# Four-layer model on one core: the third layer's feed-forward on rows sorted by expert

## The chip, the core and the metric

The kernel runs on one core of a Trainium2 chip. The metric is the time of one execution in microseconds (us), taken on the device. A core has a matrix engine (TensorE, PE), a vector engine (VectorE, DVE), a scalar engine (ScalarE, ACT), a general engine (GpSimd, POOL), and SyncE (SP), which here issues transfers. Each runs its own list of instructions in order; they wait for each other by semaphores.

## The reference

Four layers, numbered 0 to 3. In each the attention's output is multiplied by the SiLU of a feed-forward's output and added to x. Each layer has an attention and a feed-forward of its own kind. The ones that the change touches are those of layer 2, the third:

```python
# one layer: x = x + attention(layernorm(x)) * silu(feed_forward(layernorm(x))), for four layers
# x is (2, 1024, 128), FP32
def _L2_attn_ref(x, Wqkv, Wproj, bproj):
    ...
    qkv = qkv.reshape(b, n, N_HEADS, -1)
    q, k, v = (qkv[..., :dh], qkv[..., dh:2 * dh], qkv[..., 2 * dh:])
    scores = jnp.einsum('bnhd,bngd->bnhg', q, k) / SCALE
    attn = jax.nn.softmax(scores, axis=-1)
    out = jnp.einsum('bnhg,bngd->bnhd', attn, v)
    out = out.reshape(b, n, -1)
    return jnp.einsum('bni,mi->bnm', out, Wproj) + bproj

def _L2_ffn_ref(x, tile_sigs, W, b):
    ...
    pe = make_pe(S, P)
    scores = jnp.einsum('sp,tp->st', pe, jnp.sign(tile_sigs))
    idx = jnp.argmax(scores, axis=-1)
    y_all = jnp.einsum('bsd,tod->bsto', x, W) + b
    ...
    out = jnp.take_along_axis(y_all, idx4, axis=2)[:, :, 0]
    return out
```

The attention of layer 2 is a softmax over 16 heads within each position, so every position stands alone. Its feed-forward multiplies each position by one of eight 128x128 matrices. Which one follows from the position's number alone and is the same in both halves of the batch. Layers 0, 1 and 3 have feed-forwards in which the tokens choose among eight experts (two of them in 0 and 1, one in 3). Layer 3's attention is a causal product with a decay, without a softmax.

## The kernel before

The 2048 positions lie as 16 tiles of 128, in four chunks c = 0 to 3 of 512 columns (two for each half h of 1024 positions). There is one function for each engine, and in it a generator for each stage. `follow()` reads a string of words for each engine (`ORDER_A`, `SIDE_B` beside layer 0's attention, then `ORDER_C`); a word such as `ffn2.1` or `tile.12` runs that stage up to its next `yield`. These strings, written out, are the only thing that sets the order on an engine. Waits name what is waited for (`at("xnT", 2, c)`), and PSUM banks come from a ring of three, banks 4, 6 and 7.

The routed feed-forwards (layers 0, 1 and 3) work on sorted rows, in six groups: q = 0, 1 for layer 0, q = 2, 3 for layer 1, q = 4, 5 for layer 3, each a half of the positions. For a group DVE computes for every token its expert and its place in the sorted order (`route.q`, in it `counted`), and POOL scatters the normalised rows to the DRAM buffer `xsort` with indirect transfers, 128 rows each. SP loads them in tiles of 256 rows (`xrows.q`). PE transposes a tile (`xturn.q`), multiplies it by the weights of the experts of its two halves of 128 rows (`up.q`, `down.q`), and SP stores the results to `ysort` (`store.q`). Then POOL gathers each token's rows back with indirect transfers (`gather.q`), and ACT applies the SiLU. Sorted rows are padded so that each half of a tile has one expert. SP also loads the experts' weights, by a number read from the table `rt`.

The feed-forward of layer 2 works differently, by masked products. `position` computes a one-hot choice for the 1024 positions, split into three bf16 parts, in `gTT2`. `ffn2.c` runs over the eight experts of a chunk. PE spreads the row of the one-hot over 128 partitions (bf16, 128x512), DVE multiplies it with the normalised activations (`psum_sb<-xnT,ps`), and PE multiplies the product by the expert's matrix and adds up in bank 5 (`ps<-psum_sb,on_sb`). Three bf16 products add the bias, and ACT applies the SiLU into `gT`. `end2.c` then multiplies the attention's output by `Wproj`, DVE adds `bproj` and multiplies by `gT`, four transposes on PE turn the result, and DVE adds it to x.

The attention of layer 2 runs in 16 stages `tile.i`. PE makes q, k and v; ACT copies them out; DVE forms the products of q and k (128x2048) and sums them to scores (128x256) with their maxima; POOL subtracts the maxima (the shift, 128x256); ACT takes the exponential; DVE forms the shares; POOL makes the products with v in four instructions (128x512, printed 128x4x16x8 in an order listing); PE sums them over 16 transposes (`sum_turned`); and ACT copies the result. The small buffers of a tile (q, k, v, scores, maxima) are one of two, as are the two large ones of products `pr1` and `pr2`. So the sums of tile i wait for POOL's products of tile i - 2.

Normalisation of chunk c ahead of layer l is `ln.l.c`: DVE takes moments, POOL forms the offsets, ACT scales, PE transposes, ACT copies to `xnT`. In PE's, DVE's and POOL's helpers each operation has one line: 255 is a matmul, 258 a transpose, 261 a summed transpose, 264 a tensor_tensor, 277 a reduction, 280 a cast, 298 ACT's copy, 301 its activation, 304 a transfer of SP, 318 a scatter, 323 a gather, 331 a weight load by number. A few names in the profile stand for several buffers that share memory: `ar` is a large area with most of the layers' buffers, `on_sb` holds the eight matrices of layer 2.

## Time and profile before

| | |
|---|---|
| runs | 1004.75 us median of 3 (1003.81 to 1006.44) |
| profiled execution | 1003.7 us from its first to its last instruction |
| PE busy | 920.3 us, 92% |
| DVE busy | 764.0 us, 76% |
| POOL busy | 597.9 us, 60% |
| ACT busy | 538.3 us, 54% |
| moved | 97.17 MB, 97 GB/s in the mean |

The profile gives the busy time of an engine, the duration of each instruction, and what it waited for. A row of a timeline has the start, the duration, the engine and the line, the operation with output and inputs, how many of it were joined (x4), and in brackets the idle time ahead with what ended it. "Issue" is time in which the engine waited for nothing that the profile shows. The granted clock is the part of TensorE's full clock that it was given in a stretch.

### The profile page before, as it was taken

The numbers are of one execution on the slowest core, as the hardware profiler recorded it, in microseconds if no ns is written. First come the engines' busy times: TensorE is split into PE (matmuls) and PEld (weight loads), VectorE is DVE, ScalarE is ACT, GpSimd is POOL, SyncE is SP. The second block draws the span as 40 slices with busy tenths as digits, with TensorE's granted clock in tenths as the row PEclk, the third lists the DMA queues.
The fourth block names the chain that finished last, engine by engine and source line by source line (L and its number), as shares of the span: only waits on it lengthen the run. The fifth ranks groups of instructions, "written<-read, shape, count | busy, mean of one in ns | idle before, by whom it ended". The sixth has DMA issues, their size and how long they took to land. (4 is left out here: it accounts for less than half of the span.)

```text
span 1003.7 us, 20954 instructions
## 1 busy us (share of the span) xinstructions
PE 920.3 (92%) x7704; PEld 489.4 (49%) x7713; DVE 764.0 (76%) x1332; ACT 538.3 (54%) x901; POOL 597.9 (60%) x533
## 2 busy tenths in 40 slices
PE   5799997999999999999989997899889787799997
PEld 3346563233333333333323233798788444488794
DVE  6978888888888889887888825883689998873514
ACT  1255345666766666666756775443266243274463
POOL 3660425788778777887777893123735886652333
PEclk9999998999999999999999999799999997999999
DMA  9372525111111101111101123567651200243462
GB/s 319 137 225 88 153 64 156 41 51 46 26 52 28 58 24 49 34 55 56 35 26 44 40 67 116 161 193 241 225 156 35 89 22 22 79 142 101 143 196 79
DMA packets 92308, 97.17 MB, mean 97 GB/s; under 512 B 23184, under 2 KB 68624, under 8 KB 91952
## 3 DMA queue, kind: packets, MB, share of 16 engines
q1 hardware_dynamic: 87088, 85.34, 27.8%
q0 software_dynamic: 5120, 10.50, 3.6%
q8 instruction: 63, 1.03, 0.4%
q14 instruction: 37, 0.30, 0.1%
HBM read 70.57 MB, written 24.77 MB: 95 GB/s over the span
## 5 line engine op out<-in xcount | busy, mean ns | idle before, releaser
L255 PE MATMUL ps<-ar 64*64 64x512 bf16 (+5 forms) x5312 | 538.6, 448 | 17.7 <-ACT ar L301 4.3
L255 PEld LDWEIGHTS ps<-ar 64*64 64x64 bf16 (+2 forms) x5312 | 268.5, 137 | 273.4 <-ACT ar L301 92.0
L277 DVE TENSOR_REDUCE small<-ps 128x2 f32<-128x1024 f32 (+2 forms) x276 | 307.2, 1140 | 52.0 <-PE ps L255 50.6
L301 ACT ACTIVATE ar<-ps 128x1024 f32<-128x1024 f32 (+1 forms) x304 | 285.4, 941 | 113.1 <-PE ps L255 106.5
L264 POOL TENSOR_TENSOR psum_sb<-psum_sb,ar 128x1024 f32<-128x1024 f32 x91 | 214.8, 2360 | 57.3 <-DVE on_sb L264 47.1
L264 POOL TENSOR_TENSOR ar<-ar 128x512 f32<-128x512 f32 (+1 forms) x80 | 79.2, 995 | 52.1 <-DVE ar L277 30.0
L323 POOL DMA_INDIRECT gT<-ysort,rt x48 | 46.9, 977 | 98.7 <-issue 97.7
L264 DVE TENSOR_TENSOR ar<-ps,ar 128x256 f32<-128x256 f32 (+4 forms) x56 | 56.2, 1011 | 47.9 <-PE ps L255 43.4
L264 POOL TENSOR_TENSOR psum_sb<-ar 128x1024 f32<-128x1024 f32 x32 | 75.9, 2372 | 16.8 <-ACT ar L301 15.6
L298 ACT COPY ar<-ps 128x256 f32<-128x256 f32 (+1 forms) x84 | 31.8, 386 | 80.8 <-PE ps L255 50.2
L255 PE MATMUL ps<-wA,xnT 128*128 128x512 f32 (+3 forms) x192 | 62.0, 447 | 5.3 <-DVE ar L264 2.7
L255 PE MATMUL ps<-ar,onesf 128*32 128x512 f32 x384 | 61.0, 593 | 0.7 <-DVE psum_sb L264 0.6
L255 PE MATMUL ps<-ar,psum_sb 128*128 x464 | 59.6, 277 | 1.1 <-DVE ar L264 0.8
L255 PEld LDWEIGHTS ps<-ar,psum_sb 128*128 128x128 f32 x464 | 56.0, 192 | 7.9 <-issue 7.6
L318 POOL DMA_INDIRECT xsort<-ar,rt x32 | 35.4, 1105 | 36.3 <-DVE rt L280 27.9
L298 ACT COPY lrow<-ps 128x512 f32<-128x512 f32 x32 | 18.8, 586 | 66.1 <-PE ps L255 66.1
L277 DVE TENSOR_REDUCE ar<-ar 128x16 f32<-128x256 f32 (+1 forms) x48 | 49.6, 1038 | 5.2 <-ACT ar L301 4.4
L255 PE MATMUL ps<-ar,ps_sb 128*128 x96 | 48.7, 602 | 0.0
L318 POOL DMA_INDIRECT xsort<-acc_sb,rt x32 | 32.5, 1016 | 20.5 <-DVE rt L280 11.1
L255 PEld LDWEIGHTS ps<-wA,xnT 128*128 128x128 f32 x192 | 29.5, 200 | 26.6 <-issue 12.0
L255 PE MATMUL ps<-on_sb,wA 128*32 128x512 f32 x256 | 35.0, 618 | 6.0 <-DVE on_sb L264 4.6
L255 PE MATMUL ps<-psum_sb,on_sb 128*128 128x512 f32 x64 | 34.4, 620 | 6.1 <-DVE psum_sb L264 5.1
(156 smaller groups left out, 1066.0 us busy)
## 6 DMA issues: line engine op xcount, KB each, us to landing
ar<-in_L_up SPq DMA_DIRECT2D x48, 384.0 KB, 4.1
ar<-in_L_b SPq DMA_DIRECT2D x32, 322.0 KB, 3.4
rec_sb<-lscr SPq DMA_DIRECT2D x64, 128.0 KB
scr<-ar SPq DMA_DIRECT2D x48, 128.0 KB, 2.1
ar<-xsort SPq DMA_DIRECT2D x40, 128.0 KB
ysort<-ar SPq DMA_DIRECT2D x40, 128.0 KB, 3.3
ar<-scr SPq DMA_DIRECT2D x32, 112.0 KB
xsort<-xs SPq DMA_DIRECT2D x12, 256.0 KB, 6.2
```

Of the source, the lines that this page charges most:

```text
L255: return self.e.matmul(o, l, r, start=start, stop=stop) if self.e else Nothing()
L264: return self.e.tensor_tensor(o, a, b, op) if self.e else Nothing()
L277: return self.e.tensor_reduce(o, a, AX.X, op, negate=True) if negate else self.e.tensor_reduce(o, a, AX.X, op)
L298: return self.e.copy(o, a) if self.e else Nothing()
L301: return self.e.activation(o, a, fn, **kw) if self.e else Nothing()
L318: return self.e.indirect_dma_start(rows, bass.IndirectOffsetOnAxis(ap=index, axis=0), i, None)
L323: return self.e.indirect_dma_start(o, None, rows, bass.IndirectOffsetOnAxis(ap=index, axis=0))
```

## The change

Layer 2's feed-forward now works on sorted rows as well. `position` gives a one-hot of the choice, PE forms the ranks from it and DVE the places (`counted("pos")`), once for both halves. `scatter2.h` on POOL sends the normalised rows of a half to the new DRAM buffer `xsort2` in eight scatters. `xrows2.h` on SP loads them in eight tiles of 256 rows, `xturn2.h` on PE turns a tile and reads the numbers of its two experts into registers, ACT copies it (`xout2.h`), `ffn2.h` makes two FP32 and two bf16 (bias) products of 128x128, ACT copies the rows (`rows2.h`), SP stores them to `ysort2` (`store2.h`), and `gather2.h` on POOL brings them back in eight gathers, behind which ACT applies the SiLU. So 16 scatters, 16 row loads, 16 stores and 16 gathers come in. The masked products on DVE and PE and the spreads go. `end2.c` makes its products with the positions on the partitions, with `bproj` added by a bf16 product, so that the transposes and one step of DVE go. The bias rows come through three small transfers `bias2` on SP. Eight transfers of 256 KB clear `xsort2` at the start of the program. The 256 KB load of the spreading table and a clearing on POOL are dropped.

In the attention of layer 2 the small buffers are a ring of three; q is read from PSUM and no longer kept, while the two large buffers stay two. The sums of tile i then wait for the products of tile i - 3. The normalised rows of layer 2 are written to `psum_sb`, which has two buffers, since the masked products are gone from it.

`ORDER_A` and `SIDE_B` are the same word for word. `ORDER_C` is another for every engine. The lines of the helpers lie four further down (259 a matmul, 262 a transpose, 268 a tensor_tensor, 308 a transfer of SP, 322 a scatter, 327 a gather, 314 the reading of numbers on PE).

```diff
+TILES2 = ((1024 + NE * (HALF - 1)) // HALF + 1) // 2
...
-STRIDE = (256, 384, None, 512)
+STRIDE = (256, 384, 128, 512)
...
-        "tile.12 route.4 tile.9 tile.10 ffn2.3 ffn2.2 ffn2.2 route.4 ffn2.2 ffn2.3 tile.11 att3.0 tile.13 ffn2.3 "
...
+        "gather2.1 gather2.1 gather2.1 gather2.1 gather2.1 gather2.1 tile.13 gather2.1 tile.12 tile.13 tile.13 tile.13 "
...
-            pe.mm(ps[:, b, :], wA[:, 384:512], oT2[c % 2]).then_inc(*filled(b, ("proj2", c)))
-            yield
-            combine(2, c, acc_sb[:, 1024:1536])
+            pe.wait_ge(*at("bias_rows_in", 0))
+            for j in range(4):
+                d_ = ps[:, b, 128 * j:128 * j + 128]
+                pe.mm(d_, oT2[c % 2][:, 128 * j:128 * j + 128], wA[:, 384:512], stop=False)
+                ins = pe.mm(d_, onesb[0:3, :], bias_rows[0:3, 1024:1152], start=False)
+            ins.then_inc(*filled(b, ("delta", 2, c)))
...
-        def ffn2(c):
-            x_ = slice(CW * (c % 2), CW * (c % 2) + CW)
-            pe.wait_ge(*at("xn", 2, c))
-            pe.wait_ge(*at("gT", "pos"))
-            for e8 in range(NE + 1):
-                if e8 < NE:
-                    b = take(ring[0])
-                    pe.wait_ge(*vacant(b))
-                    pe.mm(ps[:, b, :], cb_late[:, 128 * e8:128 + 128 * e8], gTT2[:, x_]).then_inc(
-                        *filled(b, ("spread", c, e8)))
-                    if e8:
-                        yield
-                if e8 == 1:
-                    pe.wait_ge(*vacant(5))
-                if e8 >= 1:
-                    p = e8 - 1
-                    pe.wait_ge(*at("xb", c, p))
-                    pe.mm(ps[:, 5, :], w2l[:, 128 * p:128 * p + 128],
-                          psum_sb[:, 512 * (p % 2):512 * (p % 2) + 512], start=p == 0, stop=False).then_inc(
-                        *up(("xb_used", c, p)))
-                if e8 < NE:
-                    yield
-            pe.wait_ge(*at("bias2", 0))
...
+            pe.wait_ge(*at("pos_dve", "chosen"))
+            pe.mm(ps[:, b, 0:64], below, ohs[:, 0:64])
+            pe.mm(ps[:, b, 128:192], onesb, ohs[:, 0:64]).then_inc(*filled(b, ("ranks", "pos")))
...
+        def x_turned2(h):
+            for J in range(TILES2 * h, TILES2 * h + TILES2):
+                b = take(ring[0])
+                pe.wait_ge(*vacant(b))
+                pe.wait_ge(*at(f"xsort2_in{J % 3}", J))
+                for k in range(2):
+                    ins = pe.tr(ps[:, b, 128 * k:128 * k + 128], xin2[J % 3][:, 128 * k:128 * k + 128], ident)
+                ins.then_inc(*filled(b, ("xT2", J)))
+                pe.wait_ge(*at("experts", "pos"))
+                j = 2 * (J % TILES2)
+                number2[J] = pe.numbers(nc, experts["pos"][0:1, j:j + 2], (NE - 1) * STRIDE[2])
+                yield
+
+        number2 = {}
+
+        def ffn2(h):
+            for J in range(TILES2 * h, TILES2 * h + TILES2):
+                b = take(ring[0])
+                pe.wait_ge(*vacant(b))
+                pe.wait_ge(*at("xT2_sb", J))
+                pe.wait_ge(*at("late_in", 0))
+                pe.wait_ge(*at("bias_rows_in", 0))
+                for k in range(2):
+                    d_ = ps[:, b, 128 * k:128 * k + 128]
+                    pe.mm(d_, xT2[J % 2][:, 128 * k:128 * k + 128], w2l[:, bass.ds(number2[J][k], 128)], stop=False)
+                    ins = pe.mm(d_, onesb[0:3, :], bias_rows[0:3, :][:, bass.ds(number2[J][k], 128)], start=False)
+                ins.then_inc(*filled(b, ("yrow2", J)))
+                yield
 
...
-            dve.wait_ge(*at("proj2", c))
-            dve.wait_ge(*at("ffn_act", 2, c))
-            if c > 0:
-                dve.wait_ge(*at("delta", 2, c - 1))
-            dve.stt(acc_sb[:, 1024:1536], ps[:, bank["proj2", c], :], M("bp"), gT[:, cols(c)], ALU.add,
-                    ALU.mult).then_inc(*emptied(("proj2", c), ("gated", 2, c)))
-            yield
-            combine(2, c)
+            blend(2, c)
...
-        def ffn2(c):
-            x_ = xnT[:, cols(c)]
-            for e8 in range(NE):
-                if e8:
-                    yield
-                xb = psum_sb[:, 512 * (e8 % 2):512 * (e8 % 2) + 512]
-                dve.wait_ge(*at("spread", c, e8))
-                if e8 >= 2:
-                    dve.wait_ge(*at("xb_used", c, e8 - 2))
-                elif c > 0:
-                    dve.wait_ge(*at("xb_used", c - 1, e8 + 6))
-                dve.tt(xb, x_, ps[:, bank["spread", c, e8], :], ALU.mult).then_inc(
-                    *emptied(("spread", c, e8), ("xb", c, e8)))
...
+            counted("pos")
...
             dve.wait_ge(*at("qk", i))
-            if i >= 2:
-                dve.wait_ge(*at(f"tile{k}_pool", i - 2, "av"))
+            if i >= 3:
+                dve.wait_ge(*at(f"tile{r}_pool", i - 3, "av"))
             dve.red(s, p1, ALU.add).then_inc(*up((t, i, "scores")))
...
+        def x_out2(h):
+            for J in range(TILES2 * h, TILES2 * h + TILES2):
+                act.wait_ge(*at("xT2", J))
+                if J >= 2:
+                    act.wait_ge(*at("yrow2", J - 2))
+                else:
+                    act.wait_ge(*at("scaled", 30))
+                act.acp(xT2[J % 2], ps[:, bank["xT2", J], 0:TILE]).then_inc(*emptied(("xT2", J), ("xT2_sb", J)))
+                yield
+
+        def rows2(h):
+            for J in range(TILES2 * h, TILES2 * h + TILES2):
+                act.wait_ge(*at("yrow2", J))
+                if J >= 2:
+                    act.wait_ge(*at(f"ysort2_out{J % 2}", J - 2))
+                else:
+                    act.wait_ge(*at("scaled", 30))
+                act.acp(yrow2[J % 2], ps[:, bank["yrow2", J], 0:TILE]).then_inc(
+                    *emptied(("yrow2", J), ("yrow2_sb", J)))
+                yield
+
+        def gather2(h):
+            for c in range(2 * h, 2 * h + 2):
+                for i in range(4 * (c % 2), 4 * (c % 2) + 4):
+                    act.wait_ge(*at(f"rows2_in{i}", h))
+                act.af(gT[:, cols(c)], gT[:, cols(c)], ACT.Silu).then_inc(*up(("gather_act",), ("ffn_rows", 2, c)))
...
+        def scatter2(h):
+            pool.wait_ge(*at("experts", "pos"))
+            pool.wait_ge(*at(f"clear{h}_in", 0))
+            for i in range(8):
+                c = 2 * h + i // 4
+                pool.wait_ge(*at("xnT", 2, c))
+                pool.scatter(xsort2[h], slots["pos"][:, i:i + 1], lnbuf(2, c)[:, 128 * (i % 4):128 * (i % 4) + 128]
+                             ).then_inc(*landed(("sorted2", h) if i == 7 else ("sorted2",)))
+                yield
+
+        def gather2(h):
+            for J in (TILES2 * h + TILES2 - 2, TILES2 * h + TILES2 - 1):
+                pool.wait_ge(*at(f"ysort2_out{J % 2}", J))
+            for i in range(8):
+                pool.wait_ge(*at("x", 2, 2 * h + i // 4))
+                pool.gather(gT[:, 128 * (8 * h + i):128 * (8 * h + i) + 128], ysort2[h], slots["pos"][:, i:i + 1]
+                            ).then_inc(*landed((f"rows2_in{i}", h)))
+                yield
...
+            for r in range(0, TILES2 * TILE, 512):
+                sp.dma(xsort2[h][r:r + 512, :].rearrange("(p t) d -> p t d", p=128), xs[:, 0:4, :]).then_inc(
+                    *landed((f"clear{h}_in",)))
...
+        def bias2():
+            sp.wait_ge(*at("bias2", 0))
+            sp.wait_ge(*at("scaled", 31))
+            for i in range(3):
+                sp.dma(bias_rows[i:i + 1, 0:1152], bp2[i][0:9, :]).then_inc(
+                    *landed(("bias_rows_in", 0) if i == 2 else ("bias_rows_in",)))
+            yield
+
+        def x_rows2(h):
+            sp.wait_ge(*at("sorted2", h))
+            for J in range(TILES2 * h, TILES2 * h + TILES2):
+                r = TILE * (J - TILES2 * h)
+                if J >= 3:
+                    sp.wait_ge(*at("xT2", J - 3))
+                sp.dma(v3(xin2[J % 3], 128), xsort2[h][r:r + TILE, :].rearrange("(k p) d -> p k d", p=128)).then_inc(
+                    *landed((f"xsort2_in{J % 3}", J)))
+                yield
+
+        def store2(h):
+            for J in range(TILES2 * h, TILES2 * h + TILES2):
+                r = TILE * (J - TILES2 * h)
+                sp.wait_ge(*at("yrow2_sb", J))
+                sp.dma(ysort2[h][r:r + TILE, :].rearrange("(k p) d -> p k d", p=128), v3(yrow2[J % 2], 128)).then_inc(
+                    *landed((f"ysort2_out{J % 2}", J)))
                 yield
 
```

Three places in the order. The first is SP's, where it passes from group 2 to group 3 (`ysort<-ar` is a store, `ar<-xsort` a load of sorted rows, `in_L_up` the experts' weights). Before:

```order
L304 DMA ysort<-ar 128x2x128
L304 DMA ar<-xsort 128x2x128 x2
L304 DMA ysort<-ar 128x2x128
L329 TENSOR_LOAD rt
L331 ISA
L331 DMA ar<-in_L_up 128x768
L329 TENSOR_LOAD rt
L331 ISA
L331 DMA ar<-in_L_up 128x768
L304 DMA ysort<-ar 128x2x128
```

After the change:

```order
L333 TENSOR_LOAD rt
L335 ISA
L335 DMA ar<-in_L_up 128x768
L308 DMA ar<-xsort 128x2x128 x3
L308 DMA ysort<-ar 128x2x128 x2
L308 DMA ar<-xsort 128x2x128 x2
```

The last two stores of group 2 stood apart, with row and weight loads of group 3 between and ahead of them; now they stand together behind three row loads.

The second is POOL's, around the scatters of `route.4` (`xsort<-rec_sb,rt` and `xsort<-lrow,rt`; a 128x256 row is the shift of a tile, the 128x4x16x8 rows are products with v). Before:

```order
L264 TENSOR_TENSOR ar<-ar 128x4x16x8 x4
L264 TENSOR_TENSOR ar<-ar 128x256
L318 DMA xsort<-rec_sb,rt 3072x128 x4
L318 DMA xsort<-lrow,rt 3072x128 x4
L264 TENSOR_TENSOR ar<-ar 128x4x16x8 x4
L264 TENSOR_TENSOR ar<-ar 128x256
L264 TENSOR_TENSOR ar<-ar 128x4x16x8 x4
```

After the change:

```order
L268 TENSOR_TENSOR ar<-ar 128x4x16x8 x4
L268 TENSOR_TENSOR ar<-ar 128x256
L322 DMA xsort<-rec_sb,rt 3072x128 x4
L322 DMA xsort<-lrow,rt 3072x128 x4
L268 TENSOR_TENSOR ar<-ar 128x4x16x8 x2
L327 DMA gT<-ysort,rt 128x128 x7
L268 TENSOR_TENSOR ar<-ar 128x256
L327 DMA gT<-ysort,rt 128x128
L268 TENSOR_TENSOR ar<-ar 128x4x16x8 x6
```

The scatters of `route.4` keep their place after the shift of tile 12. Behind them, seven gathers of `gather2.1` (`gT<-ysort,rt`) stand in the middle of tile 12's four products, and one behind tile 13's shift.

The third is PE's, around the rank products of `route.4` (`ps<-rt,cb`). `ps<-osb,ar` is a spread and `ps<-psum_sb,on_sb` a masked product; in the change `ps<-cf,acc_sb` turns a sorted tile, `ps<-on_sb,rec_sb` and `ps<-osb,cb` are its product and its bias, TENSOR_LOAD and ISA read the experts' numbers. Before:

```order
L255 MATMUL ps<-wA,xnT 128x8 x8
L261 MATMUL ps<-cf,ar 128x128 x32
L255 MATMUL ps<-osb,ar 128x512 x2
L255 MATMUL ps<-psum_sb,on_sb 128x512
L255 MATMUL ps<-rt,cb 128x64 x2
L255 MATMUL ps<-psum_sb,on_sb 128x512
L255 MATMUL ps<-osb,wA 128x512 x3
```

After the change:

```order
L265 MATMUL ps<-cf,ar 128x128 x32
L262 MATMUL ps<-cf,acc_sb 128x128 x2
L314 TENSOR_LOAD rt
...
L259 ISA
L259 MATMUL ps<-on_sb,rec_sb 128x128
L259 ISA
L259 MATMUL ps<-osb,cb 128x128
L259 MATMUL ps<-rt,cb 128x64 x2
L262 MATMUL ps<-cf,acc_sb 128x128 x2
```

Behind the 32 summed transposes of two tiles, the ranks stood behind two spreads and one masked product. Now three tiles of `xturn2.1` and three of `ffn2.1` stand ahead of them.

## Rows read from the trace of the kernel before

**Rows 1.** The profile's page: busy time by engine, and a line of its DMA issues.
```profile
PE 920.3 (92%) x7704; PEld 489.4 (49%) x7713; DVE 764.0 (76%) x1332; ACT 538.3 (54%) x901; POOL 597.9 (60%) x533
...
ysort<-ar SPq DMA_DIRECT2D x40, 128.0 KB, 3.3
```

**Rows 2.** Busy time by stretch: PE, PEld, DVE, ACT, POOL, then clock, DMA share, GB/s.
```profile
738.50:782.51 44.01, 41.73 (x305) 35.56 (x308) 41.76 (x59) 26.41 (x50) 26.86 (x30) 1.00 0.34 96
782.51:865.28 82.77, 60.65 (x267) 35.62 (x271) 76.42 (x136) 28.64 (x56) 58.69 (x67) 0.94 0.11 33
...
878.77:948.06 69.29, 69.23 (x468) 56.54 (x469) 38.18 (x90) 38.01 (x103) 26.88 (x32) 1.00 0.40 121
948.06:997.30 49.24, 48.97 (x338) 40.16 (x336) 13.13 (x27) 26.77 (x91) 15.15 (x16) 1.00 0.50 147
```

**Rows 3.** Timeline of POOL, 702 to 745: start, duration, instruction, idle time ahead.
```profile
702.92 1.00 POOL L323 DMA_INDIRECT gT<-ysort,rt  x1 [14.92 <-issue]
...
722.71 1.84 POOL L323 DMA_INDIRECT acc_sb<-ysort,rt  x1 [0.30 <-issue]
...
738.50 0.62 POOL L264 TENSOR_TENSOR ar<-ar 128x256 f32<-128x256 f32 x1 [11.55 <-DVE ar L277]
742.17 2.23 POOL L264 TENSOR_TENSOR ar<-ar 128x512 f32<-128x512 f32 x2 [3.05 <-DVE ar L264]
```

**Rows 4.** The chain of waits, 683 to 703: start, duration, what.
```profile
687.05 3.10 DMA xsort<-ar,rt
...
694.89 5.00 DMA ysort<-ar
```

**Rows 5.** Timeline of SP, its DMA issues, 690 to 700.
```profile
690.17 0.90 SPq L304 DMA_DIRECT2D ar<-xsort  x2
...
699.31 0.38 SPq L304 DMA_DIRECT2D ysort<-ar  x1
```

**Rows 6.** Instructions by line and shape, 738 to 866: count, busy us, mean ns, idle ahead.
```profile
L264 POOL TENSOR_TENSOR ar<-ar 128x512 f32<-128x512 f32 x48 | 52.0, 1083 | 16.0 <-DVE ar L264 13.6
...
L264 DVE TENSOR_TENSOR psum_sb<-xnT,ps 128x512 f32<-128x512 f32 x26 | 17.3, 678 | 2.1 <-remote 2.1
...
L264 POOL TENSOR_TENSOR ar<-ar 128x256 f32<-128x256 f32 x13 | 8.5, 654 | 23.5 <-DVE ar L277 23.4
L323 POOL DMA_INDIRECT acc_sb<-ysort,rt x8 | 8.4, 1050 | 3.5 <-issue 3.5
```

**Rows 7.** Instructions on the tile psum_sb, 745 to 900: durations min/median/max.
```profile
L255 PE MATMUL ps<-psum_sb,on_sb x64: 592/592/1061, 766.0 to 890.5; 128*128 128x512 f32 x64
...
L264 DVE TENSOR_TENSOR psum_sb<-xnT,ps x32: 658/679/689, 754.8 to 883.9; 128x512 f32<-128x512 f32 x32
```

**Rows 8.** Timeline of POOL, 865 to 881.
```profile
865.28 1.10 POOL L318 DMA_INDIRECT xsort<-rec_sb,rt  x1 [3.26 <-DVE rt L280]
...
874.27 0.95 POOL L318 DMA_INDIRECT xsort<-lrow,rt  x1 [0.30 <-issue]
875.24 5.13 POOL L264 TENSOR_TENSOR ar<-ar 128x512 f32<-128x512 f32 x5
```

**Rows 9.** Timeline of PE, five places between 695 and 911.
```profile
695.47 1.50 PE L255 MATMUL ps<-ar,psum_sb 128*128 x12
...
728.78 0.63 PE L258 MATMUL ps<-cf,rec_sb 128*128 128x128 f32 x4 [4.30 <-ACT rec_sb L301]
...
834.89 3.62 PE L261 MATMUL ps<-cf,ar 128*128 128x128 f32 x16
...
875.93 1.12 PE L255 MATMUL ps<-psum_sb,on_sb 128*128 128x512 f32 x2
...
908.51 1.91 PE L261 MATMUL ps<-cf,ar 128*128 128x128 f32 x16
```

**Rows 10.** The chain of waits at the end, 995 to 999.
```profile
995.94 2.62 DMA gT<-ysort,rt
```

**Rows 11.** Busy time and granted clock, 835 to 840; columns as in Rows 2.
```profile
835.00:840.00 5.00, 4.95 (x22) 4.17 (x22) 2.82 (x3) 3.46 (x7) 3.73 (x6) 0.60 0.10 40
```

More of the change, by code:

```diff
@@ L867, in tail0 @@
                 yield
-        def combine(layer, c, a):
-            b = take(ring[0])
-            pe.wait_ge(*vacant(b))
-            pe.wait_ge(*at("gated", layer, c))
-            for j in range(4):
-                ins = pe.tr(ps[:, b, 128 * j:128 * j + 128], a[:, 128 * j:128 * j + 128], ident)
-            ins.then_inc(*filled(b, ("delta", layer, c)))
         def end0(c):
@@ L1133, in tensor_program @@
                   "end0": end0, "end1": end1, "end2": end2, "tables": tables, "rec": rec, "position": position,
[L1134 removed]
+                  "ffn2": ffn2, "xturn2": x_turned2, "tile": tile, "att3": att3, "end3": end3, "route": route}
         follow(ORDER_A["tensor"], stages)
@@ L2278, in pool_program @@
         beside(attention(), SIDE_B["gpsimd"], {"end0": end0, "ln": ln, "route": route, "gather": gather})
-        follow(ORDER_C["gpsimd"], {"clear2": clear2, "ln": ln, "tile": tile, "route": route, "gather": gather})
+        follow(ORDER_C["gpsimd"], {"scatter2": scatter2, "gather2": gather2, "ln": ln, "tile": tile, "route": route, "gather": gather})
     def sync_program(sp):
```

166 lines of the change are left out of this document (62 added, 104 removed), and 268 rows, old and new, of tables (ORDER_A, ORDER_C, SIDE_B).

## The prediction

> **What bounds the kernel now.** I read the page first: TensorE (PE) is busy 92% of the span [rows 1]. That says where most work is, not what the new feed-forward is worth, for the edits lie after about 613 us. So the table of stretches comes next [rows 2]. From 738.50 to 865.28, where the sixteen attention tiles of layer 2 run, VectorE (DVE) is busy 41.8 + 76.4 = 118.2 of 126.8 us, PE 102.4 and GpSimd (POOL) 85.6: DVE is the bound. From 878.77 to 997.30 PE is busy 118.2 of 118.5 us: layer 3 is bound by PE. What joins the two is found in POOL's timeline: its scatters for the first expert group of layer 3 (`route.4`) begin at 865.28, the eighth starts at 874.27, and PE has the first sorted rows at 878.77, where the next stretch of the table begins [rows 2, 8]. The last 6.4 us are the tail of gathers. So I time three places: G, the first gather of group 2 (702.92) [rows 3], S, the first `route.4` scatter (865.28), and the end. G to S is 162.4 us, S to the end 138.4.
>
> **What goes and what comes, by engine.** DVE loses 32 products of 0.679 us, 21.8 us [rows 7]; 26 of them (17.3 us) stand between 738 and 866 [rows 6]. PE loses the 64 FP32 products behind them, 0.592 us each by the record [rows 7], though two are done in 1.12 us, 0.56 each [rows 9]: about 35 us, and 32 bf16 spreads. It gets back 32 transposes, 32 FP32 products of 128x128 and 32 bf16 ones: at 0.12 us each (sixteen in 1.91 [rows 9]) some 12 us. POOL gets 16 scatters and 16 gathers. Eight issues from 865.28 to 874.27 are 1.28 us apart [rows 8], sixteen from 702.92 to 722.71 are 1.32 apart [rows 3]; an undisturbed one takes 0.95 and the gap of 0.30 behind it, 1.25. That is 40 us, or 42 by the dearest spacing. ScalarE (ACT) gets 32 copies of 128x256, under 0.5 us each, against 71.7 us without work between 738.50 and 865.28 [rows 2]; SP's queue has the room as well. The eight clearing transfers at the very start delay weight loads used tens of microseconds later; I cost them at nothing, and up to 2 us if that cover is gone.
>
> **Step 1, G: -6.0 (from -9 to -2).** Now the last two stores of group 2 stand on SP behind rows and weights of group 3: SP asks for those rows at 690.17 and issues the last store at 699.31; 3.6 us later, at 702.92, POOL starts [rows 3, 5]. The last `down.2` stands behind group 3's first tile on PE (the product at 695.47 [rows 9]). In the changed order both last `down.2` precede `xturn.3`, and SP holds three row loads and then both stores. From 690.15, where the scatters have landed (687.05 + 3.10 [rows 4]), that is 1.4 us for three loads (0.45 each [rows 5]), 0.9 for two stores, a landing between 3.3 (the page's median [rows 1]) and 5.0 (this place [rows 4]), so 4.15, and 0.3: 696.9, that is 6.0 earlier. It is -2 if PE's last `down.2` comes 4 us later than I think, and -9 with the short landing and PE ready before the row loads are asked for.
>
> **Step 2, G to S: +7.7, from 162.4 to 170.1.** S stands behind all of POOL's work in one queue, so it is POOL's chain that counts. Before: 35.6 us from G to tile 0's shift; from there 85.6 busy, 5.4 of gaps at sixteen gathers (3.5 of them at the eight into acc_sb [rows 6]), and 2.0 of gaps under 0.3 us: 93.0 of work, and 33.8 idle. Most of the idle time is put down to DVE's maxima (23.4) and shares (13.6, a part inside the small gaps) [rows 6]. After: the first four scatters fit into the 11.55 us that POOL waits before tile 0's shift [rows 3]; on DVE that tile's steps stand behind two more steps of the expert feed-forward, which gives the shift 2.5 us later, 38.1 after G. Of the other 28 indirect transfers 20 stand before S: 20 x 1.25 = 25.1 us, so 118.1 of work. If POOL never idled, S would come at G + 156. Walking through both orders with the durations of these rows, I still find it waiting 3.1 for tile 0's shares (as the 3.05 at 742.17 [rows 3]), 3.2 at tile 1, 1.2 for the last stores before `gather2.0`, 1.6 at tile 11, 2.7 for the slots of `route.4` (3.26 now [rows 8]) and 2.1 in short waits: 13.9 in all, with 8 and 20 as its ends. 38.1 + 118.1 + 13.9 = 170.1. The slots come late for a reason of order: on PE the rank product of `route.4` now stands behind three `xturn2.1` and three `ffn2.1`, which need the last scatter of `scatter2.1`, and everything behind that product on PE waits with it. The time that DVE loses is thus no gain by itself: it shortens a wait of POOL's, and POOL's added work takes that wait's place. The ring of three lets DVE's sums run a tile further ahead of POOL's products; its effect is in the 13.9.
>
> An issue beside a busy DVE may be dearer: the eight gathers into acc_sb in the tile stretch take 1.05 us [rows 6], an undisturbed one 0.95, so 0.1 x 20 = 2 us. I take none of it, since most of the new ones stand in runs of three to eight. The dearest single one took 1.84 us [rows 3]. The Trainium skill, "SBUF — State Buffer", section "Who interferes with whom", speaks against this change: GpSimd can't write the descriptors of its DMA while VectorE holds the port pair that they share. By its figure of 620 ns becoming 3100 ns, twenty issues would add about 50 us, an estimate from that page. The trace shows the effect at 0.1 us in the mean and doesn't bear the figure out.
>
> **Step 3, S to the end: +1.1, from 138.4 to 139.5.** PE is saturated here, so its own work and new holes count. Of the old feed-forward six products stand behind `xturn.4`, 6 x 0.56 = 3.4, with a spread and the combining transposes 1.2 more; the new form of `end2` gives 0.7 back: -3.9. The tail loses 1.5: group 5's gathers lie fully under the last attention step of layer 3, where before their landing of 2.62 us came after PE's work [rows 10]. Holes: POOL issues seven `gather2.1` between the two halves of tile 12's product, where before all four and the next shift ran on from 875.24 [rows 8]. That is 7 x 1.25 = 8.8 us; PE comes to tile 12's transposes 21.9 after S and has them 25.4 after: +3.5. `ln.3.2` stands between PE's steps so that its rows come late; one such lateness cost 4.30 at 728.78 [rows 9], nothing is the other end, and I take 2.0. Layer 3's attention is spread differently, +1.0 (0 to 1.7). Sum: -3.9 - 1.5 + 3.5 + 2.0 + 1.0 = +1.1.
>
> **Sum.** -6.0 + 7.7 + 1.1 = +2.8 on a span of 1003.7: 1006.5. The median of the runs (1004.75) stands 1.0 above the profiled span, so 1007.5.
>
> **The rivals.**
> *A, the forecast:* POOL becomes the bound of the tile stretch, 1007.5, own range 1002 to 1012. Chance 0.41.
> *B, faster:* POOL's 33.8 idle us take in the 25.1, for they are waits for DVE, which has 17 us less to do. It decides when POOL idles no more than 6 us there: S is again 162.4 after G. If the holes at tile 12 and `ln.3.2` aren't there either, the later tiles being ready sooner, the end moves by -3.9 - 1.5 + 1.0 = -4.4: 1004.75 - 6.0 - 4.4 = 994.3. For it: 33.8 exceeds 25.1. Against: a part of the waits is the way from DVE to POOL to ACT and back within a tile, which no work taken from DVE shortens. Chance 0.28.
> *C, slower by the clock:* between 738.50 and 865.28 PE was busy 102.4 of 126.8 us, and with 25 less it is near 60%. Where it was least busy, the granted clock from 835 to 840 was 0.60, and sixteen summed transposes took 3.62 us against 1.91 [rows 9, 11]. If the lower level (1.2 GHz) holds at the rank product, the first tiles of layer 3 and tile 12, 7 us of such work take 7 more: 1014.5. Against: at other times before S PE has cover. Chance 0.16. The Trainium skill, "TensorE: Matmul & The Clock Gate", section "Part 1: The HAM clock gate (the "warmup" mystery)", puts it so: "the default state is throttled, and activity releases the throttle". The row at 835 agrees.
> *D, nothing:* the earlier G is used up, since the tiles wait for DVE's normalisation and not for POOL's queue; -3.9 - 1.5 stand against +3.5 + 2.0 in the end: about 1004. Chance 0.12.
> *E, issues blocked by DVE:* at the dearest row, 1.84 against 0.95, twenty of them add 17.8: 1025. Against it stands the mean. Chance 0.03.
>
> **The numbers.** A measurement of this kernel tells 0.3%, 3 us, from no change. Faster than 1001.7: B 0.27 and 0.06 of A and D, 0.33. Slower than 1007.8: A 0.15, C 0.15, E 0.03, 0.33. Between: 0.34. The range takes in the centres of B and C: 993 to 1015.
>
> **What would show it.** The last `ysort` store of group 2 issued by 694 and G near 697; between tile 0's shift and S POOL with 118 us of work and 12 to 16 idle, S at 866 to 870, DVE under 85% busy; seven `gather2.1` before tile 12's last products, with PE idle some 3 us there. The forecast is wrong if an indirect transfer costs over 1.3 us, if POOL still idles 25 us (S is then past 878) or under 8, or if the stretch's granted clock falls below 0.8.

## The result, and the profile after

The changed kernel takes 1047.14 us (median of 4, 1045.08 to 1049.8) against 1004.28 for the one before beside it (1003.76 to 1006.44): ratio 1.0433, 95% interval 1.0415 to 1.0451. The forecast was 1007.5, with a range to 1015. Its profiled execution spans 1046.7 us, 43.0 more than before. Of the page:

```profile
span 1046.7 us, 21211 instructions
...
PE 932.0 (89%) x7751; PEld 509.0 (49%) x7751; DVE 750.9 (72%) x1308; ACT 550.9 (53%) x933; POOL 628.7 (60%) x564
...
PEclk9899998999999999999999999989996667999899
```

DVE has less work than before, POOL more, as intended. PE has 12 us more, for 7751 products and transposes against 7704 [rows 1], many of them short ones. The last line is the granted clock in 40 slices of the span, in tenths; it has a hollow of 0.6 in the slices 31 to 33, from 785 us on. The page of the kernel before has 0.9 and more in those slices and nothing under 0.7 anywhere:

```profile
PEclk9999998999999999999999999799999997999999
```

The same three places as in the forecast: G is at 696.73, S at 883.70, the end at 1046.7. SP's queue ahead of G, and POOL's queue at three places (start, duration, operation, idle time ahead and what ended it):

```profile
691.90 1.41 SPq L308 DMA_DIRECT2D ar<-xsort  x3
693.35 0.98 SPq L308 DMA_DIRECT2D ysort<-ar  x2
```

```profile
732.79 0.62 POOL L268 TENSOR_TENSOR ar<-ar 128x256 f32<-128x256 f32 x1 [4.48 <-DVE ar L281]
...
800.73 5.68 POOL L268 TENSOR_TENSOR ar<-ar 128x512 f32<-128x512 f32 x4 [7.35 <-PE ps L265]
...
875.02 5.12 POOL L268 TENSOR_TENSOR ar<-ar 128x512 f32<-128x512 f32 x5 [2.58 <-DVE ar L268]
...
883.70 1.00 POOL L322 DMA_INDIRECT xsort<-rec_sb,rt  x1 [3.57 <-DVE rt L284]
885.01 0.96 POOL L322 DMA_INDIRECT xsort<-rec_sb,rt  x1 [0.30 <-issue]
```

| | before | forecast | after |
|---|---|---|---|
| G | 702.92 | 696.9 | 696.73 |
| G to S | 162.4 | 170.1 | 187.0 |
| S to the end | 138.4 | 139.5 | 163.0 |

So step 1 came out in its number, step 2 is short by 16.9 us and step 3 by 23.5. The table of stretches (length; busy time of PE, PEld, DVE, ACT, POOL; granted clock, DMA share, GB/s) shows both. Below it stand PE's longest waits ahead of S, and DVE's steps (`ps<-ps,gT` and `xs<-xs,ps`, the multiplication and the addition to x) that end the two longest:

```profile
883.70:903.30 19.60, 18.43 (x77) 12.85 (x77) 5.42 (x11) 4.34 (x12) 12.80 (x13) 0.74 0.63 196
903.30:1041.10 137.80, 124.03 (x797) 100.33 (x796) 54.30 (x116) 69.50 (x198) 48.34 (x54) 0.96 0.37 109
732.79:792.00 59.21, 51.69 (x357) 42.80 (x356) 44.84 (x59) 31.32 (x65) 42.42 (x46) 0.92 0.45 141
792.00:883.70 91.70, 51.88 (x244) 39.03 (x244) 61.40 (x110) 29.84 (x65) 62.46 (x72) 0.70 0.15 43
```

```profile
807.73 3.67 PE L265 MATMUL ps<-cf,ar 128*128 128x128 f32 x16 [2.55 <-DVE ar L268]
...
828.30 1.12 PE L262 MATMUL ps<-cf,psum_sb 128*128 128x128 f32 x4 [10.14 <-DVE xs L268]
...
843.23 1.65 PE L259 MATMUL ps<-wA,xnT 128*128 128x384 f32 x2 [11.49 <-DVE xs L268]
...
856.92 3.68 PE L265 MATMUL ps<-cf,ar 128*128 128x128 f32 x16 [5.95 <-DVE ar L268]
```

```profile
826.82 0.70 DVE L268 TENSOR_TENSOR ps<-ps,gT 128x512 f32<-128x512 f32 x1 [6.73 <-ACT gT L305]
827.55 0.69 DVE L268 TENSOR_TENSOR xs<-xs,ps 128x512 f32<-128x512 f32 x1
...
841.75 0.70 DVE L268 TENSOR_TENSOR ps<-ps,gT 128x512 f32<-128x512 f32 x1
842.49 0.69 DVE L268 TENSOR_TENSOR xs<-xs,ps 128x512 f32<-128x512 f32 x1
```

From 792 to S no engine is busy for more than 68% of the stretch (POOL 62.46 of 91.70, DVE 61.40, PE 51.88), and the clock is 0.70: engines wait for each other. From PE's first sorted rows (903.30) to its last product it has 797 products where before had 803 from 878.77 to 997.30 [rows 2], but takes 137.80 us and not 118.5; it is busy 124.03, and idle 13.77 where it was idle 0.3. What it idles for there (wait, total us, times, longest):

```profile
PE ps L259 <- DMA ar<-in_L_b: 5.9, 6, 2.1
PE ps L262 <- DMA ar<-xsort: 3.5, 1, 3.5
PE ps L259 <- DVE ar L268: 1.6, 1, 1.6
PE ps L259 <- ACT ar L302: 1.5, 2, 1.0
```

### The profile page after: what moved, and what is told of

It is laid out like the page before. It is cut to its first block and busy times, and to the rows that moved or that the text cites. A ratio compares the mean times of both kernels' runs of the same rounds, so it can differ in the third digit from the quotient of the medians.

```text
span 1046.7 us, 21211 instructions
## 1 busy us (share of the span) xinstructions
PE 932.0 (89%) x7751; PEld 509.0 (49%) x7751; DVE 750.9 (72%) x1308; ACT 550.9 (53%) x933; POOL 628.7 (60%) x564
## 5 line engine op out<-in xcount | busy, mean ns | idle before, releaser
L259 PE MATMUL ps<-ar 64*64 64x512 bf16 (+4 forms) x5312 | 542.2, 448 | 26.1 <-DMA ar<-in_L_b 5.9
L327 POOL DMA_INDIRECT gT<-ysort,rt x64 | 61.7, 965 | 111.5 <-issue 109.3
L268 DVE TENSOR_TENSOR ar<-ps,ar 128x256 f32<-128x256 f32 (+4 forms) x56 | 56.5, 1012 | 77.2 <-PE ps L259 64.4
L268 POOL TENSOR_TENSOR psum_sb<-ar 128x1024 f32<-128x1024 f32 x32 | 75.9, 2370 | 14.6 <-ACT ar L305 13.5
L265 PE MATMUL ps<-cf,ar 128*128 128x128 f32 x256 | 39.3, 320 | 13.5 <-DVE ar L268 8.5
L259 PEld LDWEIGHTS ps<-wA,xnT 128*128 128x128 f32 x192 | 28.9, 199 | 39.5 <-DVE xs L268 12.6
L265 PEld LDWEIGHTS ps<-cf,ar 128*128 128x128 f32 x256 | 36.7, 169 | 17.5 <-DVE ar L268 8.8
L322 POOL DMA_INDIRECT xsort<-acc_sb,rt x32 | 32.7, 1022 | 19.9 <-DVE rt L284 10.4
```

The source lines that it names most:

```text
L259: return self.e.matmul(o, l, r, start=start, stop=stop) if self.e else Nothing()
L265: return self.e.matmul(o, i, idn, start=start, stop=stop, is_transpose=True) if self.e else Nothing()
L268: return self.e.tensor_tensor(o, a, b, op) if self.e else Nothing()
L322: return self.e.indirect_dma_start(rows, bass.IndirectOffsetOnAxis(ap=index, axis=0), i, None)
L327: return self.e.indirect_dma_start(o, None, rows, bass.IndirectOffsetOnAxis(ap=index, axis=0))
```

## The experiments

Times are medians with the ratio to the kernel before beside it, and its 95% interval; spans are of the profiled executions. Single executions of one kernel lie some us apart (the kernel before took 998.2 to 1007.8 us), so the ratios say whether two kernels differ, and the spans say where.

**Without POOL's issues, and with them alone.** In the first kernel `scatter2.h` and `gather2.h` keep their steps on POOL but issue nothing, and SP moves the same bytes, unsorted:

```diff
-                pool.scatter(xsort2[h], slots["pos"][:, i:i + 1], lnbuf(2, c)[:, ...]).then_inc(...)
+                sp.dma(xsort2[h][128 * i:128 * i + 128, :], lnbuf(2, c)[:, ...]).then_inc(...)
```

> The changed kernel, but the 16 scatters and 16 gathers of layer 2's feed-forward are not indirect transfers of POOL: the same rows of 128 positions are moved straight (not sorted) by direct transfers that SP issues, so the sorting is left out and POOL is free of them. Queue theory (POOL's 32 issues of 1.25 us in its one queue are the cost): POOL's stretch from tile 0's shift to the first route.4 scatter falls from 151 to 120-130 us, the whole to 1005-1018. Clock theory (TensorE works at 1.2 GHz between 782 and 900, because its masked products are gone): PE has as little to do as in the changed kernel, so the granted clock stays near 0.6 in the tile stretch and the time at 1035 or more. Order theory (the new orders hold PE and POOL at waits wherever the transfers come from): 1035 or more as well.

1041.65 us, ratio 1.0402 (1.0338 to 1.0467), span 1038.6; G to S 184.9, S to the end 158.2. The second is the kernel before with 32 scatters more on POOL, of rows that nobody reads:

```diff
+        def load2(n):
+            ...
+                pool.scatter(dump[i % 16], slots[2][:, i % 8:i % 8 + 1], w2l[...]).then_inc(...)
```

> The kernel before, with 32 indirect scatters of 64 KB of constant data into unused buffers added to POOL's queue, at places that answer to those of the changed kernel (4 ahead of tile 0, 4 around tile 3, 12 around tiles 7 and 8, 4 around tile 10, 8 between the first and second product pair's place of tile 12). The masked products on PE and DVE stay. Queue theory: the first route.4 scatter comes 15 to 25 us later, and with the eight in tile 12's place the whole is 25 to 40 us slower, 1030 to 1045, though PE keeps its clock. Clock and order theories: POOL's 34 idle us take most of the 25 in, and the whole moves by at most 12 us, to 1016.

1031.71, ratio 1.0303 (1.0234 to 1.0372), span 1028.3; G to S 177.1 and S to the end 148.8. In the old orders 32 issues, with the transfers that they start, cost 24.6 us of span; by the ratio it is 30, from 23 to 37. In the new ones taking them out gives 8.1 of span, but by the ratios only some 3, and the intervals (1.0338 to 1.0467, 1.0415 to 1.0451) overlap: what it is worth there isn't settled, only that it leaves most of the loss. POOL then idles instead.

**The clock.** Fillers on TensorE, into a bank that nothing reads before its next real write, first 71 FP32 products of 128x512:

```diff
+        def warm(n, k):
+            pe.wait_ge(*at("late_in", 0))
+            for _ in range(n):
+                pe.mm(ps[:, 5, :], w2l[:, 0:128], w2l[:, 0:512])
```

> The changed kernel with FP32 products of 128x512 that nobody reads added on PE into the unused PSUM bank 5: 5 single ones between the sorted tiles of the first half, 20 and 24 where PE waits 10.1 and 11.5 us for DVE (818 to 843), 12 and 10 in the later waits up to 875. Clock theory: the granted clock between 792 and 884 rises from 0.6 - 0.8 to over 0.9, and the time falls by 12 us or more, to 1035 or less. Queue theory: the clock rises, but POOL's chain stays, and the time stays within 5 us of 1047.

1064.37, ratio 1.0629 (1.0551 to 1.0707). The clock was 1.00 from 782 to 803 us and 0.94 from there to 900, and POOL's wait before its products at 800 us shrank from 7.35 to 0.79, but fillers of 0.86 us each in front of real work cost more than that. The other way to that wait, the sums of tiles 4 and 5 earlier on PE and ACT:

```diff
-... ffn2.0 ffn2.0 xturn2.0 tile.6 ffn2.0 xturn2.0 ... rec.3 rec.3 tile.4 tile.5 tile.7
+... ffn2.0 ffn2.0 tile.4 xturn2.0 tile.6 ffn2.0 xturn2.0 tile.5 ... rec.3 rec.3 tile.7
```

> The changed kernel with the summed transposes of tiles 4 and 5 moved ahead on PE and ACT (behind the second and the sixth product of ffn2.0 in place of behind rec.3), where POOL's products for them are done. Order theory: POOL's wait of 7.35 us for PE at 793 goes, the first route.4 scatter comes 6 to 8 us earlier, and the whole is at 1041 or less. Queue theory: the same wait goes, but the gathers behind it wait for stores and DVE's steps, so half of it at most reaches the scatter: 1043 to 1047.

1049.86, ratio 1.0484 (1.0399 to 1.0569), span 1050.6: the wait went and S came at 889.23. That wait by itself is not what holds S. Then some 260 short fillers, fitted into the waits:

```diff
+            for _ in range(n):
+                pe.mm(ps[:, 5, 0:384], onesb, cb[:, 0:384])
```

> The kernel after with about 290 extra small products on TensorE (128x384, BF16 operands, into bank 5, which nothing reads before the next real write), in 17 groups placed just where TensorE waited between 733 and 885 us in the kernel after. Unlike the FP32 ones of the earlier run they are short, so each delays a real instruction by little; the groups fill the waits but are not longer than them at the full clock. Nothing is left out. Theory 'the low granted clock': the clock stays at the full level from 733 to 885, the sixteen summed transposes take 1.9 to 2.0 us instead of 3.6, route.4's first scatter falls at G+172 to G+177 (after: G+187.0) and the span ends at 1020 to 1030 us (after: 1046.7). Rival 'POOL's queue and the waits on it': the clock rises but S stays at G+185 or later and the time at 1045 or more. Rival 'the fillers only delay': slower than 1050.

1040.13, ratio 1.036 (1.0313 to 1.0407), span 1040.1, G to S 185.1, S to the end 158.8. In the places of the longest waits the table reads:

```profile
820.00:860.00 40.00, 37.61 (x230) 23.61 (x229) 26.67 (x49) 16.84 (x32) 31.69 (x42) 1.00 0.12 34
860.00:884.00 24.00, 21.57 (x141) 14.91 (x139) 18.86 (x42) 7.00 (x20) 16.80 (x19) 1.00 0.26 77
```

The clock is up from 801 to 886 us, but the expected gain of about 20 us didn't come: it is 7 (by the medians, and by the ratios 1.0433 and 1.036). From POOL's products at 800 to S it is 79.0 against 83.0, from S to the end 158.8 against 163.0. PE idles as long after its first sorted rows as in the kernel after: 14.1 of 134.2 us. With the issues off POOL as well, by the first diff of this section:

> As the run before it, and the sixteen scatters and sixteen gathers of the sorted positions are taken off POOL's queue and made direct transfers on SP's (the positions are then not sorted, so the third layer's tables and expert choice no longer fit them and the output differs; every transfer, product and wait is still there). It measures what POOL's queue costs when the clock is not low. If clock and queue are two separate prices, the time is 5 to 10 us under the run before it (about 1013 to 1023 us), since taking the queue off alone gave 5. If the clock is the whole of the loss, it is within 3 us of the run before. If the queue is what holds the kernel once the clock is up, it falls by 15 or more, to 1010 or below, near the kernel before.

1040.61, ratio 1.0401 (1.0342 to 1.046), span 1037.3, G to S 181.8: no gain that the ratios tell from the run before it. The fillers were fitted to waits that end some 5 us sooner without the issues (PE goes on at 823.79 and 837.71 in the first kernel of this section, for 828.30 and 843.23). Here 66 of them stand ahead of the transposes at 827.08 with no wait left, so the run gives at best a lower bound for the issues. The last of this kind, FP32 fillers up to 785 us and short ones behind:

```diff
+            if k < 6:
...
+                pe.mm(ps[:, 5, :], w2l[:, 0:128], w2l[:, 0:512])
+            else:
+                for _ in range(n):
+                    pe.mm(ps[:, 5, 0:384], onesb, cb[:, 0:384])
```

> The kernel of the small fillers once more, but its first six groups, among the second feed-forward's small products up to 785 us, are each one FP32 product of 128x512 (0.86 to 1.1 us) as in the first filler run, in which the clock stayed up from 783 to 801. Nothing is left out. It puts the clock up at both places. The runs so far price the low clock by place: POOL's wait for TensorE before its products at 800 us was 7.35 in the kernel after, 9.66 with the small fillers (clock still low there), 0.79 with the FP32 ones; from those products to S it was 83.0 us in the kernel after and 79.0 with the small fillers; from S to the end 163.0 and 158.8. If these add up, the clock is worth 6.5 + 4.0 + 4.2 = 15 us less what the fillers delay (2 to 4): S at G+176 to G+180 and a span of 1031 to 1036. Rival 'the wait at 800 is not on the path' (turning the order there round gave nothing): S at G+184 or later and the span at 1039 or more. Rival 'the clock is the whole loss': 1015 or less.

1039.8, ratio 1.035 (1.031 to 1.0389); the profiled execution was the longest of five, span 1045.4. In it the clock was 0.51 from 791 to 798 all the same and the wait at 801 stood at 7.50. It says nothing on that wait, and repeats the 7 us.

**What taking the masked work away is worth.** The kernel before, thinned:

```diff
+                    n = 64 if p else 512
-                    pe.mm(ps[:, 5, :], w2l[:, 128 * p:128 * p + 128], psum_sb[..., 512 columns], ...
+                    pe.mm(ps[:, 5, 0:n], w2l[:, 128 * p:128 * p + 128], psum_sb[..., n columns], ...
...
+                n = 64 if e8 else 512
-                dve.tt(xb, x_, ps[:, bank["spread", c, e8], :], ALU.mult)
+                dve.tt(xb[:, 0:n], x_[:, 0:n], ps[:, bank["spread", c, e8], 0:n], ALU.mult)
```

> The kernel before, with its masked feed-forward made thin and nothing put in its place: 28 of its 32 products on VectorE and the 56 FP32 matmul passes behind them work on 64 columns instead of 512, so seven of eight experts contribute to only an eighth of the positions; every instruction, wait, order and transfer of the kernel before stays. It measures what taking the work away is worth with the old orders and without POOL's new queue. VectorE loses about 28 x 0.45 = 12.6 us and TensorE about 28 x 0.9 = 25 us between the gathers of group 2 and S. Theory 'work taken from VectorE shortens the waits of POOL, but the clock takes a part back': G to S 153 to 158 (before 162.4), granted clock of that stretch below 0.93, span 994 to 999. Rival 'TensorE's lower load brings the clock down for good, and with it the kernel': the span is 1004 or more. Rival 'pure gain, no clock effect': 993 or less with the clock at 0.96 or more in the stretch.

1005.41, ratio 1.0017 (0.9993 to 1.004), span 1001.2: next to nothing. From tile 0's shift to S, and from PE's first sorted rows on:

```profile
733.81:861.38 127.57, 97.49 (x570) 77.25 (x569) 108.79 (x194) 54.74 (x104) 85.56 (x98) 0.86 0.18 54
...
874.80:994.80 120.00, 119.27 (x804) 98.98 (x804) 50.20 (x116) 64.65 (x194) 42.14 (x48) 0.97 0.45 130
```

DVE lost 9.4 us of its 118.2 in the stretch [rows 2], and the stretch is 0.8 longer than before (G to S 160.5 against 162.4). POOL did the same 85.6. DVE's busy share said bound, and less work on DVE brought nothing. One rival is left: with less on PE the granted clock of the stretch is 0.86, where by [rows 2] it was 0.96, and the slower products may have taken back a part of what DVE gave. No run thins DVE's work alone. For the change the sum of both counts, since it takes the work from both engines.

**The ring.** 

> The kernel after with one part undone: the small buffers of layer 2's attention (scores, maxima, sums, keys and values of a tile) are again a ring of two, not of three; orders, sorted feed-forward and all else as in the kernel after. Nothing is left out. Theory 'the ring is a small help': VectorE's sum of a tile again waits for POOL's last product two tiles before, 1 to 4 us longer, 1048 to 1051. Rival 'the ring is worth nothing in this order': within 1 us of 1046.7. Rival 'the ring lets VectorE run ahead of what is late and does harm': under 1045.

```diff
-            k, r = i % 2, i % 3
+            k, r = i % 2, i % 2
...
-                dve.wait_ge(*at(f"tile{r}_pool", i - 3, "av"))
+                dve.wait_ge(*at(f"tile{r}_pool", i - 2, "av"))
```

1050.07, ratio 1.0463 (1.0416 to 1.051), which overlaps that of the kernel after. G to S is 189.3 against 187.0, as expected, but the span is 1047.3. The medians are 2.9 us apart: whether the ring helps isn't settled.

**Both halves of the work, old orders; and the new orders without the work.** The first is the thinned kernel before with the 32 scatters, that is the diffs of `load2` and of the thinning together.

> The kernel before with both sides of the change and none of its orders: the masked feed-forward thinned as in the run before (28 of 32 products of VectorE and 56 matmul passes at 64 columns, so seven of eight experts reach an eighth of the positions), and 32 extra indirect scatters on POOL into buffers that nothing reads, at the places of the earlier run. Alone, the thinning was worth 2.5 us of span (1001.2) and the issues cost 24.6 (1028.3). Theory 'work taken from VectorE and TensorE does not pay for POOL's issues, and the orders of before are better than the new ones': 1023 to 1029, well under the 1046.7 of the kernel after. Rival 'what VectorE gives back covers the issues' (the forecast's second rival): 1012 or less. Rival 'with both, TensorE's clock falls as in the kernel after, and that is the loss': 1035 or more, with the granted clock under 0.85 between tile 0's shift and S.

1027.62, ratio 1.0252 (1.0206 to 1.0298), span 1027.7, which is 0.6 under the run with the issues alone. By the ratios it is 5, with intervals that overlap: the freed DVE and PE time pays at most a small part of the issues.

> The kernel after with the sorted feed-forward of layer 2 left as a shell: no scatter or gather on POOL (direct transfers on SP instead, positions unsorted, as in an earlier run), its matmul passes at 16 columns instead of 128 and its copies on ScalarE cut to 16 and 32 columns; the waits, the transfers, the ring of three and the orders stay. It is the partner of the thinned kernel before (1001.2 us): both have next to no feed-forward in layer 2, and they differ in the orders, the ring and the waits along the sorted path. Theory 'the loss lies in the new orders and their waits, more than in the work of the sorted feed-forward': 1034 to 1040. Rival 'the small products and copies on TensorE and ScalarE are the loss': 1020 or less. Rival 'all of the loss is POOL's issues': 1005.

```diff
-                    d_ = ps[:, b, 128 * k:128 * k + 128]
+                    d_ = ps[:, b, 128 * k:128 * k + 16]
```

1036.24, ratio 1.035 (1.0298 to 1.0401), span 1034.9, G to S 181.2, S to the end 158.5. No issue of the new scatters or gathers, almost no product or copy, and still 33.7 over its partner, the thinned kernel before (span 1001.2). The two differ in the orders, but also in the ring, the new form of `end2`, the clearing, and the transfers and waits of the sorted path. Its table, and the two waits on PE that the kernel after has at 828 and 843 (its helpers lie one line further down):

```profile
731.21:876.38 145.17, 104.65 (x601) 84.99 (x599) 105.69 (x169) 56.46 (x129) 84.69 (x98) 0.76 0.29 87
...
895.75:1030.20 134.45, 121.89 (x797) 98.14 (x796) 54.14 (x116) 69.28 (x198) 43.37 (x49) 0.97 0.38 110
```

```profile
821.09 1.11 PE L263 MATMUL ps<-cf,psum_sb 128*128 128x128 f32 x4 [5.79 <-DVE xs L269]
...
835.01 1.65 PE L260 MATMUL ps<-wA,xnT 128*128 128x384 f32 x2 [10.48 <-DVE xs L269]
```

POOL's work is the 85 us of the thinned kernel to within 1 us (84.69 and 85.56), DVE's is less, and the stretch is 145.17 against 127.57. From S to PE's first sorted rows it is 19.4 (before 13.5), and behind them PE idles 12.6 us against 0.7.

**Other orders.** Only `ORDER_C` changed: some words of each engine are moved by a few places. On POOL, behind `route.4` (runs of a word written with its count):

```diff
-tile.12 gather2.1*7 tile.13 gather2.1 tile.12 tile.13*3 tile.12 ln.3.2 tile.15 tile.14*2 tile.15*3
+tile.11 tile.12 gather2.1*5 tile.13 gather2.1*3 tile.12 tile.13*2 ln.3.2 tile.15 tile.14*2 tile.15*2
```

> The kernel after with nothing changed but ORDER_C: from layer 2's first tiles on, words of all five engines are moved by some places, chosen with the durations that the rows of the traces give and TensorE at its full clock. By that sum S comes 4.9 us sooner after G and S to the end is 7.4 us shorter, 12.3 in all. Theory 'the orders are the larger part of the loss, and the clock stays low whatever the order': a span of 1032 to 1038, still well above the kernel before, with the granted clock between tile 0's shift and S again near 0.8. Rival 'fewer waits of TensorE bring the clock up as well': 1025 or less. Rival 'the order is not what holds it': within 3 us of 1046.7.

1038.45, ratio 1.034 (1.0301 to 1.0379), span 1036.9, G to S 181.2, S to the end 156.2. The expected 12.3 came out as 9.8 of span (5.8 and 6.9, less a G that is 2.9 later). The clock between tile 0's shift and S is 0.78, against 0.79 in the kernel after, so this gain is that of the order.

## Why the prediction was wrong

**Where the 43.0 us are, as far as shown.** From 1003.7: both halves of the work in the old orders bring 24.0 (to 1027.7), and since the thinning alone brings nothing, these are POOL's issues. The remaining 19.0 are found by difference: the new orders with the waits of the sorted path and the lower clock that goes with them. Of these, other orders alone gave 9.8 back. Seen from the other side, the shell costs 33.7 over the thinned kernel, and the work and issues that it leaves out 11.8 more (1034.9 to 1046.7). The two don't add up in one way, for POOL's issues partly lie in the waits that the orders make.

**Step 1, G: the number right, by some luck.** 696.73 for 696.9. The order on SP did what was worked out: three row loads and then both stores. But two terms were off and cancelled. SP began at 691.90 and not at 690.15, and its stores were issued by 694.33, 1.9 later than the sum has them; the last of them landed 2.5 us after its issue and not 4.15.

**Step 2, G to S: the step that failed is the idle time of 13.9.** Tile 0's shift came 36.1 after G (38.1). POOL's work behind it, busy time and issue gaps, was 115.8 (118.1), and an issue was 0.95 + 0.30 as taken. But POOL idled 35.1, over the 20 that I gave as its end. Before it idled 33.8: of the 24.6 by which G to S grew, 22.8 are POOL's added work, and the idle time that should have taken in 20 of them didn't shrink at all. Of the 35.1, 7.35 is the wait for PE at 800.73, 8.4 the waits at tiles 0 and 1 (6.3 forecast), 10.6 those after 844 us (4.3 forecast for tile 11 and the slots, 3.26 of it before), the rest short ones. The view behind the step was wrong in both directions: that DVE is the bound, and that POOL becomes it once it has 118 us of work. The thinned kernel gives DVE 9.4 us back and gains nothing (at a lower clock); the kernel with direct transfers gives POOL its issues back and S comes only 2.1 us sooner after G. As I read the rows, what sets S is a round through four engines. POOL gathers rows, ACT applies the SiLU, DVE multiplies and adds them to x (`xs`), and only then is a bank of PE's ring of three free. At 828 it is the bank of `end2.0`, whose rows `gather2.0` brings; PE needs it to turn chunk 2. At 843 it is the bank of `end1.3`, whose rows `gather.3` brings and which DVE handles only behind four steps of tile 8; PE needs it for q, k and v of tile 9. PE stands still 10.14 and 11.49 us there, in the shell 5.79 and 10.48. I had walked POOL's and DVE's queues against each other, and PE's bank ring not at all. That the bank and these two waits are the cause of the full 16.9 is argued from the rows; no run took them away alone.

**The clock, rival C: there, and of the size that the rival gave.** The stretch from 792 to S had 0.70, and sixteen summed transposes took 3.67 as against 1.91 [rows 9]. The rival gave 7 us. The fillers got back 7.0 of median (1047.14 to 1040.13), net of what they delay, so some 7 is a lower bound for the clock between 801 and 886; after the result I had taken it for about 20, and the runs with short fillers didn't bear that out. The Trainium skill, "TensorE: Matmul & The Clock Gate", section "Part 1: The HAM clock gate (the "warmup" mystery)", says that activity releases the throttle. The full clock between 801 and 886 us of the run with short fillers agrees. Both signs of being wrong on this stretch were there: its clock is 0.79 from tile 0's shift to S, under 0.8, and S is past 878.

**Step 3, S to the end: the step that failed is "PE is saturated here".** It gave 1.1; it is 24.6. PE's first sorted rows come 19.6 after S and not 13.5 (+6.1). The rest of `xturn2.1` and `ffn2.1` stands there on PE, at a clock of 0.74, and SP asks for the rows behind the stores of `store2.1`; but the shell, which has almost none of these products, needs 19.4 as well. From there 13.77 idle against 0.3 (+13.4), 5.9 of it for the experts' loads (`in_L_b`) and 3.5 for the sorted rows of group 5, and 5.8 more busy time for six products fewer. The tail is 5.65 against 6.4 (-0.8): I had it 1.5 shorter. I costed holes at tile 12, `ln.3.2` and the attention, 6.5 in all, and took the transfers to be hidden as before. The shell, without an issue at tile 12, needs 158.5, so the seven gathers there are not the main loss; the kernel with fillers needs 158.8 at a clock of 0.98, so the clock is a small part of it, some 4.2. By exclusion the rest is the orders, with the waits that they make. Which words, is open: the run with other orders got 6.9 of the 24.6 back.

**The other rivals.** B, that POOL's idle time takes the issues in, is refuted by the thinned kernel with issues: 1027.7, where the expectation gave it 1012 or less. D named no loss. E fell: the issues were 0.95 us beside a busy DVE. The Trainium skill, "SBUF — State Buffer", section "Who interferes with whom", doesn't speak against the change as the prediction has it: it ties the blocking to VectorE's two-port modes, which `tensor_tensor` doesn't have and `tensor_reduce` can't enter on trn2. DVE's work between G and S is mostly these two, and the 0.95 us agree.

## What to carry to other kernels

Before a change that takes work from the busiest engine, make that work thin and leave everything else: here one run showed that 9 us of DVE's time in the stretch, with PE's share of the same work, were worth nothing. An engine at 93% in a stretch can still be one stop of a round; add up the round, with the banks that PE holds, and not one queue. An order written out by hand is a part of the kernel's time: when a stage changes engines, cost the new order by itself, from PE's idle time behind it as well as ahead of it.

## What the runs showed of the hardware that I had not expected

TensorE's clock fell while it was busy. In the kernel after, the stretches from 764 on read:

```profile
764.00:776.00 12.00, 10.63 (x87) 9.69 (x87) 9.99 (x13) 5.25 (x13) 9.39 (x11) 1.00 0.47 134
776.00:782.00 6.00, 4.54 (x22) 2.73 (x22) 3.33 (x3) 1.39 (x4) 4.36 (x6) 1.00 1.05 369
782.00:799.00 17.00, 14.53 (x41) 8.44 (x42) 6.71 (x11) 3.67 (x11) 9.69 (x10) 0.51 0.29 85
```

PE was busy 14.53 of 17 us at half clock, in pairs of 128x128 products with waits of 0.65 to 1.0 us between them, and had been busy 4.54 of 6 ahead of that. With five FP32 products of 128x512 among them the clock was 1.00 in the same stretch, with short bf16 fillers alone it was 0.53 from 783 to 801, PE busy for 16.10 of the 18 us. Neither kind is a recipe: in the run with six FP32 products and the short ones behind, the clock was 1.00 from 780 to 791 and 0.51 from 791 to 798. And an indirect issue on POOL costs its 1.25 us in full where POOL is the one that others wait for: eight of them at tile 12 in the kernel before lengthened S to the end by 10.4 us (138.4 to 148.8), and in the thinned one by 9.4 (139.8 to 149.2).
